# Cross-attention iterations: the weighing of a group joins the next run of scores and turns

## What is computed

```python
x = x + xattn(layernorm(x), ctx_4096, mask, ...)   # 8 batches, 64 queries, 256 keys, 32 heads on 8 kv heads, head size 128
x = x + attn(layernorm(x), ...)                    # causal self-attention with rotary positions
x = x + ffn(layernorm(x), ...)                     # four mixed streams, 50 Sinkhorn steps

# inside xattn, n_rep = 4
q = rmsnorm(hidden @ q_proj_w.T, q_norm_w)
k = rmsnorm(repeat(ctx @ k_proj_w.T), k_norm_w)
v = repeat(ctx @ v_proj_w.T)
attn = softmax(q @ k.T / sqrt(128) + mask)
out = (attn @ v) @ o_proj_w.T
```

## Time and profile before

| | us |
|---|---|
| median of 3 runs (lowest, highest) | 1107.49 (1107.48, 1110.83) |
| span of the profiled execution, first to last instruction | 1105.4 |
| TensorE busy in it | 1074.2 (97%) |
| VectorE busy | 812.7 |
| ScalarE busy | 482.0 |
| GpSimd busy | 198.3 |

### The profile page before, as it was taken

The page is one execution under the profiler, slowest core; times in us unless marked ns, Lnnn a source line. Parts: engine busy times, 40 slices in busy tenths (PEclk is TensorE's granted clock), DMA queues, the critical chain, the costliest instruction groups (busy, mean ns, idle before and its releaser), DMA issues.

```text
span 1105.4 us, 17806 instructions
## 1 busy us (share of the span) xinstructions
PE 1074.2 (97%) x6380; PEld 902.4 (82%) x6380; DVE 812.7 (74%) x1942; ACT 482.0 (44%) x1033; POOL 198.3 (18%) x198
## 2 busy tenths in 40 slices
PE   6999999999999999999999999999999999999688
PEld 4888888788888888888888888888888878888467
DVE  5887667666667878776668877757536798758997
ACT  4544434444445446544444455434213334431417
POOL 2000000233223233333232230000001032140001
PEclk9999999999999999999999999999999999999889
DMA  9975775244543333244455312699935614000001
GB/s 238 174 200 126 159 161 146 51 110 110 114 99 87 76 76 70 62 94 109 97 107 114 76 34 58 136 215 242 213 63 105 109 24 76 2 14 1 1 1 77
DMA packets 184542, 111.29 MB, mean 101 GB/s; under 512 B 108040, under 2 KB 174472, under 8 KB 184480
## 3 DMA queue, kind: packets, MB, share of 16 engines
q1 hardware_dynamic: 182080, 109.17, 45.8%
q10 hardware_dynamic: 2400, 1.31, 0.5%
HBM read 90.98 MB, written 18.94 MB: 99 GB/s over the span
## 4 chain that ended last, share of the span: by engine, by line
PE 94%; DVE 3%; ACT 1%; DMA 1%; issue 0%; SPq 0%; DVEq 0%
PE ps L635 32%; PE ps L535 16%; PE ps L602 14%; PE ps L983 9%; PE ps L519 4%; PE ps L663 4%; PE ps L646 4%; PE ps L971 2%; PE ps L746 1%; PE ps L936 1%; DMA raw<-in_L_xattn_q_proj_w 1%; PE ps L879 1%; PE ps L1076 1%; PE ps L864 1%; PE ps L847 1%; PE ps L943 0%
## 5 line engine op out<-in xcount | busy, mean ns | idle before, releaser
L635 PE MATMUL ps<-wt,act 128*128 128x512 f32 x1536 | 381.0, 394 | 0.0
L635 PEld LDWEIGHTS ps<-wt,act 128*128 128x128 f32 x1536 | 278.1, 188 | 51.8 <-issue 0.4
L535 PE MATMUL ps<-wt,act 128*128 128x512 f32 x768 | 179.1, 394 | 1.4 <-ACT act L1109 1.0
L535 PEld LDWEIGHTS ps<-wt,act 128*128 128x128 f32 x768 | 145.0, 190 | 33.3 <-ACT wt L1114 3.4
L602 PE MATMUL ps<-act,wt 128*128 128x512 f32 x672 | 153.7, 390 | 0.0
L1114 ACT ACTIVATE wt<-raw 128x512 fp32r<-128x512 f32 x192 | 106.6, 625 | 95.6 <-PE ps L535 52.1
L602 PEld LDWEIGHTS ps<-act,wt 128*128 128x128 f32 x672 | 125.9, 188 | 26.0
L1565 DVE STREAM_TRANSPOSE raw<-raw 128x1024 f32<-128x1024 f32 x92 | 107.9, 1216 | 22.6 <-DMA raw<-in_L_xattn_o_proj_w 22.6
L983 PE MATMUL ps<-wt,act 128*128 128x512 f32 x480 | 121.5, 400 | 0.0
L1573 DVE TENSOR_TENSOR wt<-raw,wt 128x512 fp32r<-128x512 f32 x172 | 107.4, 682 | 15.9 <-ACT wt L1114 15.8
L2391 POOL TENSOR_TENSOR small<-small 128x4 f32<-128x4 f32 (+2 forms) x64 | 69.0, 1080 | 246.1 <-DVE small L1587 200.2
(11 more groups left out here) (178 smaller groups left out, 1274.4 us busy)
## 6 DMA issues: line engine op xcount, KB each, us to landing
xr<-in_ctx SPq DMA_DIRECT2D x64, 256.0 KB, 4.9
raw<-in_L_xattn_o_proj_w SPq DMA_DIRECT2D x32, 512.0 KB, 14.6
raw<-in_L_xattn_q_proj_w SPq DMA_DIRECT2D x28, 512.0 KB, 9.2
xr<-q_rows SPq DMA_DIRECT2D x16, 512.0 KB, 4.2
ot_hi<-spare SPq DMA_DIRECT2D x64, 128.0 KB, 2.0
act<-ot_hi SPq DMA_DIRECT2D x32, 256.0 KB, 9.4
q_rows<-G SPq DMA_DIRECT2D x28, 256.0 KB, 2.7
raw<-in_L_xattn_k_proj_w SPq DMA_DIRECT2D x8, 512.0 KB, 6.9
```

The costliest lines, as they stand in the source:

```text
L535: mm = pe.matmul(banks[t], lhs(p == 2, c, t), wt[:, n_slot, int(p == 1), c, :], start=(acc_from and q == 0), stop=(acc_to and q == 3 * NC ...
L635: mm = pe.matmul(bank, src[int(p == 2)][:, c, kt * P:(kt + 1) * P], wt[:, slot, int(p == 1), c, :], start=(q == 0), stop=(q == 3 * NC - 1))
```

## The change

TensorE's list of an iteration is ordered anew. Before, the four projections were cut into ten runs, with a weigh in the middle of most of them. Afterwards each key projection and the first value projection is one run of 24, and the last is cut into 9 and 15 by the second `turn_k`; between two runs stands one block of `scores`, `weigh` and `turn_probs`. The weigh in such a block is of the group two before the scores, so the weigh of group 2 moves into the next iteration, beside that of group 3. The first `turn_k` stands right behind the fourth block.

```diff
             def iteration(i, m, carry=True):          # TensorE
                 a = i - 1
-                if carry:
-                    turn_probs(a - 1, 3, m, 1)
-                pe.wait_ge(ctx_lo, 2 * i + 1)
-                pe.wait_ge(k_normed, 2 * i - 1)
-                project(i, kacc[0], 0, 0, 0, 4)
                 pe.wait_ge(lo_done, m if carry else m + 1)
                 pe.wait_ge(q_lo, 2 * i - 1)
                 if not carry:
                     pe.wait_ge(q_sums_read, 1)
                 scores(a, 0)
-                project(i, kacc[0], 0, 0, 4, 12)
+                if carry:
+                    weigh(a - 1, 2, m - 3)
+                    turn_probs(a - 1, 3, m, 1)
+                pe.wait_ge(ctx_lo, 2 * i + 1)
+                pe.wait_ge(k_normed, 2 * i - 1)
+                project(i, kacc[0], 0, 0, 0, 24).then_inc(k_done, 1)
+                scores(a, 1)
                 if carry:
                     weigh(a - 1, 3, m)
-                project(i, kacc[0], 0, 0, 12, 24).then_inc(k_done, 1)
                 turn_probs(a, 0, m + 1, 0)
-                scores(a, 1)
                 pe.wait_ge(k_normed, 2 * i)
                 pe.wait_ge(ctx_lo, 2 * i + 2)
-                project(i, kacc[1], 1, 0, 0, 12)
+                project(i, kacc[1], 1, 0, 0, 24).then_inc(k_done, 1)
+                pe.wait_ge(q_lo, 2 * i)
+                scores(a, 2)
                 pe.wait_ge(v_lo, 2 * i)
                 weigh(a, 0, m + 1)
-                project(i, kacc[1], 1, 0, 12, 24).then_inc(k_done, 1)
                 turn_probs(a, 1, m + 2, 1)
-                pe.wait_ge(q_lo, 2 * i)
-                scores(a, 2)
-                project(i, vacc[0], 0, 1, 0, 12)
+                project(i, vacc[0], 0, 1, 0, 24).then_inc(v_done, 1)
+                scores(a, 3)
                 weigh(a, 1, m + 2)
-                project(i, vacc[0], 0, 1, 12, 24).then_inc(v_done, 1)
                 turn_probs(a, 2, m + 3, 0)
-                scores(a, 3)
-                project(i, vacc[1], 1, 1, 0, 6)
                 turn_k(i, 0, m + 4, 1)
-                project(i, vacc[1], 1, 1, 6, 12)
-                weigh(a, 2, m + 3)
+                project(i, vacc[1], 1, 1, 0, 9)
                 turn_k(i, 1, m + 5, 0)
-                project(i, vacc[1], 1, 1, 12, 24).then_inc(v_done, 1)
+                project(i, vacc[1], 1, 1, 9, 24).then_inc(v_done, 1)
```

The other lists follow:

```diff
             def iteration(...):                       # ScalarE
                 if carry:
+                    read_o(a - 1, 2)
                     hi_p(m, 1)
+                exp_s(a, 0)
                 sc.wait_ge(v_done, 2 * i)
                 hi_ctx(i, 1, ctxT)
-                exp_s(a, 0)
                 if extra:
                     extra(0)
+                square_k(i, 0)
                 if carry:
                     read_o(a - 1, 3)
                 hi_v(a)
-                square_k(i, 0)
                 if extra:
                     extra(1)
                 hi_p(m + 1, 0)
...
-                read_o(a, 0)
                 square_k(i, 1)
                 if extra:
                     extra(3)
+                read_o(a, 0)
...
                 if extra:
                     extra(4)
+                    extra(5)
                 read_o(a, 1)
-                if extra:
-                    extra(5)
...
-                read_o(a, 2)
             def iteration(...):                       # VectorE
+                read_scores(a, 0)
                 if carry:
                     lo_p(m, 1)
-                read_scores(a, 0)
                 norm_probs(a, 0)
                 if extra:
                     extra(0)
+                    extra(1)
+                read_scores(a, 1)
                 lo_v(a)
-                if extra:
-                    extra(1)
                 lo_p(m + 1, 0)
-                read_scores(a, 1)
...
+                read_scores(a, 2)
                 lo_p(m + 2, 1)
-                read_scores(a, 2)
...
+                read_scores(a, 3)
                 lo_p(m + 3, 0)
-                read_scores(a, 3)
```

More of the change, by code:

```diff
@@ L418, in iteration @@
                 if older:
+                    store_o(i - 2, 2, *older)
                     store_o(i - 2, 3, *older)
-                for g in range(3):
+                for g in range(2):
                     store_o(i - 1, g, *old)
@@ L463, in _ @@
             load_quarter(0, 1, act_loaded[0][1])
+            store_o(14, 2, 6, 1)
             store_o(14, 3, 6, 1)
@@ L748, in first_o @@
                 return mm
+            weigh(14, 2, M_TAIL - 3)
             turn_probs(14, 3, M_TAIL, 1)
@@ L1342, in _ @@
             iteration(15, 93, more=False, extra=hi_12)
+            read_o(14, 2)
             hi_p(M_TAIL, 1)
```

## The result

| | before | after |
|---|---|---|
| median, us | 1107.89 (1107.48 to 1110.83, 4 runs) | 1113.95 (1113.32 to 1114.45, 4 runs) |
| ratio | | 1.0051 [1.0039, 1.0062] |
| span of the profiled execution | 1105.4 | 1112.7 |
| first scores of iteration 1 to the start of the output projection (L535, after L537) | 703.25 - 219.56 = 483.7 | 710.45 - 219.68 = 490.8 |

The change makes the kernel 0.5% slower; 1112.0 was forecast. The profiled execution, at 1114.45 us, is the slowest of its four. The last row leaves out the head of the program (all before the first scores of iteration 1), whose length differs among the traces here by up to 2.8 us (219.39 to 222.16), so it is used from here on to compare traces.

The account below looks back on a forecast made before the run. TensorE's list plus its waits was taken as the bound. Terms -2.1 + 0.9 + 0.5 + 3.0 + 2.2 = +4.5 took the span from 1105.4 to 1109.9; the median, 2.1 over it, was 1112.0 us, range 1106 to 1116.5.

Parts of the forecast that it names:

- Starts of a run: TensorE's project runs: five fewer starts per iteration, 0.028 us each, over 15 iterations save 2.1 us.
- Iteration 1: Before the first scores: four matmuls no longer cover the wait for lo_q, +0.9 us, bounds 0.6 to 1.1.
- the late context: Iteration 1: hi_ctx(1, 1) behind exp_s(0, 0); its low part still comes about 0.2 us before the second key run.
- Iteration 7: Three low chunks on VectorE delay lo_p, so turn_k 1 begins 0.5 us later.
- Iteration 8: VectorE idles at hook 1; weigh 0.2, turn 0.7, turn_k 1 2.5 us late; less 0.4 waited before, +3.0.
- The arithmetic of the blocks: VectorE and ScalarE start times worked out from block prices; each stall held good to 0.4 us.
- the rival's mechanism: Clock falls to 1.2 GHz in iteration 8's 2.5 us gap, adding 5 us: 1117; chance 0.03.
- the forecast's own: The kernel becomes slower by the summed terms: 1109.5 to 1114.5 us with its errors; chance 0.61.
- Iteration 15: Second quarter at hook 1 comes late: weigh +0.6, turn +0.7, turn_k 1 +0.9, in all +2.2 us.
- Ordinary iterations covered: No TensorE wait in ordinary iterations; tightest at turn_k 1, where lo_p is done with 0.86 us to spare.

Follow-up runs that it names:

- run without the gaps of 8 and 15: Changed kernel with ScalarE's hook 1 right behind hook 0, hook 3 ahead of square_k(i, 1) and hi_ctx(i, 1) at the head of the iteration: 1107.24 us.
- the cut run: The run without the gaps of 8 and 15, with each first key projection cut into 8, 8 and 8: 30.35 us in iterations 9 to 12, against 30.30.
- the repair: Changed kernel with seven matmuls of the first key projection ahead of iteration 1's first scores: 28.48 us from scores 0 to 2, against 28.50.
- the run with the context first: Changed kernel with only hi_ctx(i, 1) moved to the head of ScalarE's iteration: 1117.83 us, iteration 8 35.15 us.

## Why the prediction was right

- **Direction and size.** +4.5 us on the span was forecast; +7.3 came in the profiled execution, +6.1 between the medians and +5.6 (0.51%) by the ratio. The order of the terms was right: iteration 8, then 15.
- **Starts of a run: -2.1 forecast, about -0.7 measured.** An ordinary iteration gained 0.05, not 0.14, and 15 of them make 0.75. The run without the gaps of 8 and 15 says the same: 483.9 is 0.2 over 483.7, with 0.9 lost in iteration 1, 0.4 in iteration 7, and the 0.4 gone that iteration 8 waited before: 0.2 - 0.9 - 0.4 + 0.4 = -0.7. The price of a start was right (0.025 by the cut run), the term three times too large, mostly because I took scores and weigh at their old price where they now stand side by side.
- **Iteration 1: +0.9 forecast, 1.49 - 0.59 = 0.90 measured.** That the late context had only 0.2 us to spare was in the bounds; it is what defeats the repair.
- **Iteration 7: +0.5 forecast, +0.43.**
- **Iteration 8: stalls of 0.2, 0.7 and 2.5 forecast; 0.18, 0.55 and 2.43 measured (distance between starts less its steady value).** The arithmetic of the blocks held. Two things were missing in it. GpSimd's subtraction stopped VectorE at hook 0 by 1.8 us; it did not show, because VectorE would have waited for chunk 2 anyway. And the clock fell, +1.6: the rival's mechanism beside the forecast's own, for a third of the price I gave it.
- **Iteration 15: 0.6, 0.7 and 0.9 forecast; 0.55, 0.55 and 0.87 measured**, and 33.40 us against 31.37 once repaired.
- **Ordinary iterations covered:** right. In the changed kernel `lo_p` ends 0.9 before turn_k 1 begins (334.25, 335.17), as worked out (0.86).
- **Sum**, measured, of 7.1 us up to the output projection: +0.9, +0.4, iteration 8 +2.8 in gaps (3.2 less the 0.4 of before) and +1.6 in clock, iteration 15 +2.0, saving -0.7: 7.0. The forecast of 4.5 is passed, to within 0.1, by the saving that was put too high (1.4) and by the clock (1.6), less 0.5 by which the gaps were put too high. The range for the forecast's own case, 1109.5 to 1114.5, held the median of 1113.95, but near its end: the gaps, which carry the direction, were nearly right, the saving was a third of its term, and the clock was no part of this case.

The timeline rows behind the point on ordinary iterations, changed kernel, an ordinary iteration:

```profile
333.57 0.68 DVE L1555 TENSOR_TENSOR act<-ps,act 128x512 fp32r<-128x512 f32 x1
...
335.17 0.60 PE L521 MATMUL ps<-ident,G 128*128 128x128 f32 x4
```

## What to carry to other kernels

When a step moves later on the bound engine, look at every list for work that stands behind its consumer: a hook that was free because its predecessor came early is a knot once that predecessor is late, and a tidy new order of one engine needs the hooks of the others moved with it. Work such a knot out as start times in each engine's list, row by row; sums of busy time (VectorE 74% busy) don't show it. And when a repair leaves a rest, look for the next wait underneath before blaming the load: here there were two, one hidden by the other.

## What the hardware showed that I had not expected

- A subtraction on VectorE with both inputs in SBUF took 2.48 us instead of 0.68 beside GpSimd's 2.4 us subtraction, a larger one 2.58 instead of 1.22, and the scaling L1705 in ordinary iterations 1.11 for its pair instead of 0.62. Reads of PSUM beside the same operation were not slowed (L1693 0.83 to 0.88). GpSimd pays too: in the run with the context first its 2.40 became 2.96 in iteration 8, beside the last chunks of unit 10. A wait of this kind stands in the record as busy time: the chunk (1.8 us longer), the quarter (1.4) and 13 such scalings (6.3 together) make 9.5 us of records, in part overlapping, and so answer for VectorE's 8.8 us more.
- The clock fell to 1.2 GHz for 3.41 us behind a gap of 2.3 us in two executions and stayed at 2.4 GHz in two others with a gap as long.
- Start of a run of 512-column matmuls: 0.025 us over its steady step.
